# Pieces of projections between attention tiles, fewer stack transfers, and layer norms moved from ACT and DVE to POOL, in a two-layer transformer kernel on one core

## What is computed

```python
x = layernorm(x + attn(x))        # 16 heads, 2048 x 2048 scores each, softmax, w_out
dist = softmax(mean(x @ Wr + br)) # one row per batch
idx = sort(top_k(dist, 4))
Q, K, V = (x @ W + b for the four heads idx)
x = layernorm(x + softmax(Q K^T / 8) V @ Wo + bo)
def layernorm(x): return (x - mean) / sqrt(var + 1e-5)
```

## Time and profile before

| | us |
|---|---|
| median of 3 runs | 4086.33 (4085.86 to 4088.03) |
| the profiled execution | 4086.6 |
| its span, first to last instruction | 4084.8 |
| PE busy | 3616.2 (89%) |
| DVE busy | 3287.2 (80%) |
| ACT busy | 3098.1 (76%) |
| POOL busy | 1662.8 (41%) |
| mean granted TensorE clock | 0.887 of 2.4 GHz |

### The profile page before, as it was taken

The page is one execution under the profiler, slowest core; times in us unless marked ns, Lnnn a source line. Parts: engine busy times, 40 slices in busy tenths (PEclk is TensorE's granted clock), DMA queues, the critical chain, the costliest instruction groups (busy, mean ns, idle before and its releaser), DMA issues.

```text
span 4084.8 us, 41654 instructions
## 1 busy us (share of the span) xinstructions
PE 3616.2 (89%) x13992; PEld 1329.7 (33%) x13992; DVE 3287.2 (80%) x3352; ACT 3098.1 (76%) x5069; POOL 1662.8 (41%) x1115
## 2 busy tenths in 40 slices
PE   7888888778999999788999999788999999599997
PEld 3233223223333333323333332323333322343443
DVE  7888888988989898888989898888989898543442
ACT  5888888886888889786888889786888889423333
POOL 3122332100445555400445545401445545437776
PEclk7777777678999999878999999778999999799998
DMA  5122221110000000210000000210000000100000
GB/s 159 67 75 67 83 75 62 57 45 16 16 16 19 21 21 26 67 38 16 16 16 19 26 16 26 73 33 16 16 16 25 21 16 19 53 9 1 11 11 11
DMA packets 117192, 142.62 MB, mean 35 GB/s; under 512 B 33394, under 2 KB 100466, under 8 KB 116978
## 3 DMA queue, kind: packets, MB, share of 16 engines
q1 hardware_dynamic: 116978, 139.95, 11.0%
HBM read 89.55 MB, written 50.33 MB: 34 GB/s over the span
## 4 chain that ended last, share of the span: by engine, by line
PE 47%; DVE 29%; ACT 17%; issue 5%; POOL 2%; SPq 1%; DMA 0%; POOLq 0%; DVEq 0%; ACTq 0%
DVE nmax L1083 18%; ACT ps L920 14%; PE ps L796 8%; PE ps L886 8%; PE ps L858 7%; PE ps L761 7%; PE ps L873 7%; DVE smax L1162 6%; PE ps L775 6%; POOL facc L720 2%; PE ps L876 2%; PE ps L769 1%; PE ps L894 1%; ACT probs L990 1%; DVE st L1062 1%
## 5 line engine op out<-in xcount | busy, mean ns | idle before, releaser
L920 ACT ACTIVATE ps<-ps,nmax 128x1024 f32<-128x1024 f32 x2048 | 2233.0, 1094 | 388.4 <-DVE nmax L1083 365.6
L1083 DVE TENSOR_REDUCE nmax<-ps 128x1 f32<-128x1024 f32 x2048 | 2379.4, 1216 | 135.2 <-PE ps L796 122.5
L796 PE MATMUL ps<-stack 96*128 96x512 bf16 x4096 | 1350.6, 436 | 237.0 <-ACT ps L920 149.4
L720 POOL TENSOR_TENSOR facc<-facc,probs 128x1024 f32<-128x1024 f32 x448 | 1051.2, 2346 | 550.9 <-ACT probs L990 528.8
L1162 DVE TENSOR_REDUCE smax<-ps 128x2 f32<-128x1024 f32 x512 | 616.5, 1220 | 261.3 <-PE ps L858 260.9
L796 PEld LDWEIGHTS ps<-stack 96*128 96x128 bf16 x4096 | 298.2, 102 | 1411.0 <-ACT ps L920 939.2
L990 ACT ACTIVATE probs<-ps 128x1024 f32<-128x1024 f32 x512 | 524.0, 1024 | 229.1 <-PE ps L876 227.8
L858 PE MATMUL ps<-fk,fq 64*128 64x512 f32 x2048 | 571.0, 650 | 41.4 <-ACT ps L920 38.1
L873 PE MATMUL ps<-fq,fk 64*128 64x512 f32 x2048 | 545.7, 609 | 29.0 <-ACT ps L920 27.9
L886 PE MATMUL ps<-probs,vals 128*64 128x512 f32 x2048 | 506.9, 608 | 5.0 <-ACT probs L990 4.5
L920 ACT ACTIVATION_READ_ACCUMULATOR ps<-ps,nmax 128x1 f32 x2048 | 417.0, 204 | 0.0
(11 more groups left out here) (117 smaller groups left out, 1985.5 us busy)
## 6 DMA issues: line engine op xcount, KB each, us to landing
stack<-qk_levels SPq DMA_DIRECT2D x768, 64.0 KB, 2.2
qk_levels<-fk SPq DMA_DIRECT2D x64, 384.0 KB, 2.6
probs<-in_L_attn_x SPq DMA_DIRECT2D x16, 512.0 KB, 3.8
res<-in_L_attn_x SPq DMA_DIRECT2D x16, 512.0 KB, 4.0
v_rows<-vals SPq DMA_DIRECT2D x16, 512.0 KB, 2.6
vrows<-v_rows SPq DMA_DIRECT2D x16, 512.0 KB, 3.4
x_rows<-y SPq DMA_DIRECT2D x16, 512.0 KB, 2.9
res<-x_rows SPq DMA_DIRECT2D x16, 512.0 KB, 3.9
```

Source lines behind the costliest of these rows:

```text
L720: pool.tensor_tensor(total, total, probs[:, slot, :], ALU.add).then_inc(facc_ready, 1)
L796: last = pe.matmul(bank(banks[i]), stack[0:SK, hd % 2, 0, t * P:(t + 1) * P], stack[0:SK, hd % 2, 1, col:col + CH], start=True, stop=True)
L920: act.activation(src, src, ACT.Exp, bias=nmax[:, b % 2, half, t, hd:hd + 1], scale=-1.0, accum_out=esum[:, b % 2, half, t, hd:hd + 1]).the ...
L1083: dve.tensor_reduce(nmax[:, b % 2, half, t, hd:hd + 1], two_banks(banks), AX.XY, ALU.min).then_inc(min_ready, 1)
```

## The change

It has five parts, and the plan is computed anew with all of them.

- Projections are divided on PE: QP, KP, FK, FQ and D into two pieces, VP, FV, OP and FO into four (`PARTS`). Each piece is an entry of its own in PE's lists, at the same spot; the first takes the banks, the last tells the reader. Another unit can run between two pieces.
- A head's stack comes in six DMAs instead of 12: three for the queries, in which one level is repeated over up to three parts of the stack by a broadcast source, and three for the keys.
- In the last batch DVE adds the second to fourth bank of each group straight from PSUM to oacc; ACT's copy to part and POOL's addition are gone there.
- For both norms of batches 0 to 2 POOL computes the root, from an integer first guess (one step) and three Newton steps of four instructions, and scales. The last batch keeps ACT's root with one Newton step, and DVE.
- The order of the first inputs has each XT one chunk ahead of its projections, and the plan counts PE's units of the first stage at 1.5 times their cost (`COLD`).

```diff
+NEWTON = 3
+ROOT_START = float(0x5F3759DF)
+COLD = 1.5
+PARTS = {"QP": 2, "KP": 2, "FK": 2, "FQ": 2, "VP": 4, "FV": 4, "OP": 4, "FO": 4, "D": 2}
...
-    inputs += place([u for c in chunks for u in (("XT", 0, c), ("QP", 0, 0, c), ("KP", 0, 0, c))], -3, 1)
+    ahead = [("XT", 0, 0)]
+    for c in chunks:
+        ahead += [("XT", 0, c + 1)] * (c + 1 < NCH) + [("QP", 0, 0, c), ("KP", 0, 0, c)]
+    inputs += place(ahead, -3, 1)
...
+    for units in (main, inputs):
+        units[:] = [(spot, u) for spot, t in units for u in [("part", i) + t for i in range(PARTS.get(t[0], 1) - 1)] + [t]]
...
-        name = ("PE",) + tag
-        unit(name, us, after)
-        banks_of[name], reader[name] = banks, read_by
+        parts = PARTS.get(tag[0], 1)
+        for i in range(parts):
+            name = ("PE",) + (("part", i) if i + 1 < parts else ()) + tag
+            unit(name, us / parts, after if i == 0 else [])
+            banks_of[name] = banks if i == 0 else 0
+            if i == 0:
+                reader[name] = read_by
...
-        scale = dve if k == "OP" or b == B - 1 else pool
-        unit(act("LN", *t), 3.0, [dve(*t)])
-        unit(scale("NM", *t), 2.1 if scale is dve else 6.0, [act("LN", *t)])
+        scale = dve if b == B - 1 else pool
+        root = act if scale is dve else pool
+        unit(root("LN", *t), 3.0, [dve(*t)])
+        unit(scale("NM", *t), 2.1 if scale is dve else 4.9, [root("LN", *t)])
...
-                start(n, now, cost[n] + switch)
+                start(n, now, cost[n] * (COLD if key < 0 else 1) + switch)
...
-                    for side, which in ((0, Q_LEVEL), (1, K_LEVEL)):
-                        for g, lv in enumerate(which):
-                            sp.dma_start(stack[g * AD:(g + 1) * AD, k % 2, side, :],
-                                         qk_dram[b, side, h, lv, r * AD:(r + 1) * AD, :]).then_inc(stack_in[k % 2], 16)
+                    rows = qk_dram[b, :, h, :, r * AD:(r + 1) * AD, :]
+                    for at, n in ((0, 3), (3, 2), (5, 1)):
+                        into = lambda side: stack[at * AD:(at + n) * AD, k % 2, side, :]
+                        lv = Q_LEVEL[at]
+                        sp.dma_start(into(0), rows[0, lv:lv + 1].to_broadcast([n, AD, L])).then_inc(stack_in[k % 2], 16)
+                        sp.dma_start(into(1), rows[1, 0:n]).then_inc(stack_in[k % 2], 16)
...
+                elif kind == "LN":
+                    i, base = norm_no[at], (nth[n] - 1) * ROOT_STEPS
+                    pool.wait_ge(var_ready, i + 1)
+                    if i >= 2:
+                        pool.wait_ge(n_ready[i % 2], i // 2)
+                    pool.tensor_scalar(rstd[:, i % 2, :].bitcast(I32), var[:, i % 2, :].bitcast(I32), -0.5, ROOT_START,
+                                       ALU.mult, ALU.add).then_inc(newt_pool, 1)
+                    for k in range(NEWTON):
+                        pool.wait_ge(newt_pool, base + 4 * k + 1)
+                        newton(pool, i, newt_pool, base + 4 * k + 1, root_pool if k + 1 == NEWTON else newt_pool)
...
+                elif kind == "V":
+                    b, g, q = at
+                    dve.wait_ge(pv_done, step_no(b, g, (q + 1) * BURST - 1))
+                    dve.wait_ge(part_ready, nth["ACT", "V", b, g, 0])
+                    dve.wait_ge(oacc_ready, sum_no(b, g, q) - 1)
+                    dve.tensor_tensor(oacc[:, g % 2, :], bank(held["PE", "V", b, g, q * BURST][0]), oacc[:, g % 2, :],
+                                      ALU.add).then_inc(oacc_ready, 1)
```

More of the change, by code:

```diff
@@ L469, in build @@
         order, held, freed, planned = plan()
-        fill_no = {n[1:]: i + 1 for i, n in enumerate(n for n in order["PE"] if n in held and n[1] != "V")}
+        fill_no = {n[1:]: i + 1 for i, n in enumerate(n for n in order["PE"] if n in held and n[1] not in ("V", "part"))}
         nth = {}
@@ L495, in build @@
         norm_no = {t: i for i, t in enumerate(norms)}
-        nth_norm = [nth[e, "NM", *t] - 1 for t in norms for e in ("DVE", "POOL") if (e, "NM", *t) in nth]
         a_no = lambda b, j: b * A_TILES + j + 1
@@ L648, in scale_rows @@
             eng.wait_ge(steps, done + 3)
-            eng.tensor_tensor(r, r, n, ALU.mult).then_inc(steps, 1)
-            eng.wait_ge(steps, done + 4)
+            eng.tensor_tensor(r, r, n, ALU.mult).then_inc(last, 1)
+        def scale_rows(eng, i):
+            s = i % 2
             for t in range(TPC):
@@ L755, in _, with pieces, project_rows @@
             pe.wait_ge(wT_read, 3)
-            def project_rows(banks, rowsT, w):
-                for t in range(TPC):
+            def pieces(kind, piece, count):
+                parts = PARTS.get(kind, 1)
+                return range(count * piece // parts, count * (piece + 1) // parts)
+            def project_rows(kind, piece, banks, rowsT, w):
+                for t in pieces(kind, piece, TPC):
                     for cc in range(KC):
@@ L771, in transpose_rows, with project @@
                 last.then_inc(filled, 1)
-            def project(banks, wT, columns):
-                for cc in range(KC):
+            def project(kind, piece, banks, wT, columns):
+                for cc in pieces(kind, piece, KC):
                     last = pe.matmul(bank(banks[0]), wT(cc), columns(cc), start=(cc == 0), stop=(cc == KC - 1))
-                last.then_inc(filled, 1)
+                if cc == KC - 1:
+                    last.then_inc(filled, 1)
             for n in order["PE"]:
-                kind, at = n[1], n[2:]
-                banks = held.get(n)
+                if n[1] == "part":
+                    piece, kind, at = n[2], n[3], n[4:]
+                else:
+                    piece, kind, at = PARTS.get(n[1], 1) - 1, n[1], n[2:]
+                banks = held.get(("PE", kind) + at)
                 for was in freed.get(n, ()):
@@ L785, in _ @@
                         pe.wait_ge(y_ready, norm_no[was[1:]] + 1)
+                    elif was[:2] == ("DVE", "V"):
+                        pe.wait_ge(oacc_ready, sum_no(*was[2:]))
                     else:
@@ L806, in _ @@
                     pe.wait_ge(xT_ready, i + 1)
[L807 removed]
+                    project(kind, piece, banks, lambda cc: w_inT[:, cc, s * P:(s + 1) * P], lambda cc: xT[:, i % NCH, cc, :])
                 elif kind == "VP":
@@ L811, in _ @@
                     pe.wait_ge(xT_ready, i + 1)
-                    project_rows(banks, xT[:, i % NCH, :, :], w_inT[:, :, 2 * D:3 * D])
+                    project_rows(kind, piece, banks, xT[:, i % NCH, :, :], w_inT[:, :, 2 * D:3 * D])
                 elif kind == "OT":
@@ L819, in _ @@
                     pe.wait_ge(oT_ready, b * NCH + c + 1)
-                    project_rows(banks, oT, w_outT)
+                    project_rows(kind, piece, banks, oT, w_outT)
                 elif kind == "X1":
@@ L840, in _ @@
                     pe.wait_ge(wv_in, (b + 1) * V_DMAS * 16)
-                    project_rows(banks, x1T[:, :, c * CH:(c + 1) * CH], wv_sel)
+                    project_rows(kind, piece, banks, x1T[:, :, c * CH:(c + 1) * CH], wv_sel)
                 elif kind == "FO":
@@ L844, in _ @@
                     pe.wait_ge(foT_ready, group_no(b, PAIRS * c + PAIRS - 1) + 1)
-                    project_rows(banks, foT[:, :, c * CH:(c + 1) * CH], wo_sb)
+                    project_rows(kind, piece, banks, foT[:, :, c * CH:(c + 1) * CH], wo_sb)
                 else:
```

55 lines of the change are left out of this document (33 added, 22 removed).

## The result

The changed kernel takes 4099.00 us (median of ten runs, 4088.01 to 4101.36), beside 4086.19 (4085.28 to 4088.43) for the kernel before in the same series. The ratio is 1.0027 with a 95% interval of 1.0018 to 1.0036: a quarter of a per cent slower, where 2.5% faster was predicted. The profiled execution has a span of 4098.6 us, 13.8 more than before.

What follows compares the result with a forecast made beforehand. The first stage was taken as bound by DVE's work plus holes torn by whole projections, later stages by PE. Terms -4 - 42 - 42 - 9 - 3 - 4 = -104 us took 4086.6 to 3983 us, range 3915 to 4065.

Steps and rivals of the forecast that it cites:

- PE takes a tile between pieces whenever a pair of banks is free and the tile is due: First stage: tiles run between pieces of divided projections, so 60% of DVE's 70.3 us of waits go, -42 us.
- rival 5: Whole kernel: the plan shifts work but pieces come due together, time within 8 us of before; chance 0.05.
- The start: Before the first tile: transposes one chunk ahead and fewer stack DMAs to issue, -4 us, ends -7 and 0.
- The first stage: Batch 0's attention tiles, 60 to 711 us: divided projections close 60% of DVE's waits for VP and QP, -42 us.
- rival 1: PE is next at once: a third of the first stage's holes closes, -40 in all, 4047 us; chance 0.15.
- The wait for VP under 20 us: Sign of success in the first stage: DVE's wait before the VP copy falls from 47.5 to under 20 us.
- a mean clock under 0.6 in the first stage: Sign of being wrong: PE's mean granted clock in the first stage, 0.72 before, falls under 0.6.
- rival 3: First stage: cut-up runs keep PE at 1.2 GHz, deciding under mean clock 0.58; +110 us there, 4135 us; chance 0.08.
- The boundaries: Three stretches between PE-bound stages: division -11 and norms moved to POOL -3, so -14 each, -42 us in all.
- rival 2: POOL's longer norm chain sets the boundaries: -3 each, -9 for -42, 4016 us; chance 0.15.
- PE-bound stages: Three stages of the second attention: PE's idle time shrinks a little, -3 each, -9 us; ends -15 and +6.
- The last batch and the tail: From 3625 us on: DVE adds products from PSUM, -3 in the batch; three POOL additions leave the tail, -4.

Runs made afterwards that it cites:

- e3_whole: The changed kernel with all projections whole again (PARTS empty), all else as changed: 4115.31 us, ratio 1.0069 to the kernel before.
- e2_cold_one: The changed kernel with COLD at 1 in place of 1.5: 4081.14 us, ratio 0.9986 to the kernel before.
- f2_before_cold: The kernel before with only PE's first-stage work priced at 1.5 in the plan: 4097.40 us, ratio 1.0024.
- g1_apart_not_last: The changed kernel with twelve stack DMAs a head, COLD 1, and later pieces (except D's) at later spots, but not in the last batch: 4024.64 us.
- e1_twelve_dmas: The changed kernel with the old twelve stack DMAs a head in place of six: 4090.01 us, ratio 1.0004 to the kernel before.

## Why the prediction was wrong

**The step that failed** is the sentence "PE takes a tile between pieces whenever a pair of banks is free and the tile is due". It carries -42 us of the first stage and -33 of the boundaries. The plan takes the ready unit with the lowest spot, all pieces of a projection have one spot, and once the first is lower than the next tile, so are the rest. Only a piece taken ahead of its turn got another unit behind it. In the change 6 of the 112 pieces of QP, KP and VP that have a seam behind them are such, and none of the 6 got one; with COLD at 1 it is 48, of which 39 got one. Both the rule and the diff's "(spot, u) ... for u in" were in front of me. I had even named the case, as the bound "pieces come due back to back" and as rival 5, "The plan shifts the work but pieces come due together, so little changes", and gave it 0.05. Its mechanism is what happened in the first stage, where not one seam of QP, KP or VP was filled.

Point by point, forecast against what was measured:

- **The start**, -4: measured +4.2. The order of the transposes and the first issue did gain (first tile at 52.9 with twelve DMAs, 4.6 earlier: -4 was near for that part, though no run has the order alone). "If one costs the same to issue" missed the real cost. What mattered was not the issue but the transfer: three engines instead of sixteen. The issues were slower too, 0.4 to 0.9 us each and later 2.3 and 2.4. My upper bound for the start was 0, and a slower transfer was not in it.
- **The first stage**, -42: measured +23.3. The division gave 0 (e3_whole). What cost it is COLD, which I read as a detail of the order and gave no price: -20.7 when undone (e2_cold_one), +13.2 in the plan of before (f2_before_cold). With 66 of the 112 seams of that stage filled it is 23.3 us under before (g1_apart_not_last), about the third that rival 1 assumed, not the 60% that I took. So the term would have been nearly twice too large even with the mechanism at work in these seams. The wait for VP under 20 us that I named as a sign measured 23.2, but COLD brought it there and not the division: it is 23.2 in e3_whole too.
- **The clock**. The sign of being wrong was "a mean clock under 0.6 in the first stage": it rose, to 0.82. That does not test rival 3 yet, as the runs of VP were still whole. Cut up in g1_apart_not_last, the clock is 0.74, well over its 0.58, and rival 3 is out. But a higher clock was no gain: PE was quicker and then waited longer.
- **The boundaries**, -14 each: the periods, boundary and PE-bound stage together, gave -4.9, -6.9, -3.0, where -17 each was forecast. The holes before the norms and before the values' copy, which carried the -11, stayed as they were (13.6 and 9.9 us, before 12.2 and 10.0), since no seam of OP and FV was filled; with 13 and 21 of 48 filled, g1_apart_not_last waits 4.2 us for OP behind J1 and has no line for FV there. I summed division and norms (-3) as if each stood for itself. The norms alone give nothing; their lead is lost by the next J unless some pieces give as well.
- **POOL's chain**, rival 2: the 13 steps of 3.7 us and 4.8 us of scaling came as worked out (3.8 and 4.83), and PE's wait for y is 0.8 to 1.5 us in a boundary, under the 3 us that I had named. Rival 2 is out.
- **Table loads**: 64 before, 16 in the two lines of L1018 and L1020, as predicted, and ACT is 73 us less busy. It bought what the periods show and no more.
- **PE-bound stages**, -3 each: 0. From the first group's maximum to the next J it is 672.8, 672.9 and 672.4 us, before 672.7 in all three. So neither the -3 nor the +6 was seen.
- **The last batch and the tail**, -3 and -4: J3 to the end was +1.0. The part ahead of the first group's maximum became 2.8 longer (132.7, before 129.9), what follows it 1.8 shorter. Three lines of POOL's timeline in the tail show what was gained:

```profile
4038.71 2.35 POOL L752 TENSOR_TENSOR facc<-probs 128x1024 f32<-128x1024 f32 x1 [6.94 <-ACT probs L1036]
4041.20 34.74 POOL L755 TENSOR_TENSOR facc<-facc,probs 128x1024 f32<-128x1024 f32 x14
4079.94 0.61 POOL L769 COPY frec_wide<-frec 128x512 f32<-128x512 f32 x1 [4.00 <-DVE frec L1231]
```

The additions of oacc are gone from between those of facc, as predicted. From the first facc to the copy of frec it is 41.2 us, before 43.3 (4021.29 to 4064.60): 2.1 saved, not 3.8. Before, the third addition lay beside D's matmuls and cost nothing.

The ledger of the spans, forecast against found:

```
                          forecast   found
division, first stage        -42       0     e3_whole: tile stage 735.9, after 735.8
division, boundaries         -33     -17.0   whole periods, after less e3_whole
norms                         -9      +2.2   whole periods, e3_whole less before
PE-bound stages               -9       0     after less before, in the two rows above
COLD                           -      +20.7  e2_cold_one
rest of the tile stage         -      +2.6   e2_cold_one 715.1, before 712.5
start                         -4      +4.2   of it the wide DMAs +8.8, e1_twelve_dmas
last batch and tail           -7      +1.0
sum                         -104     +13.7
```

## What to carry to other kernels

When a change cuts work so that something else can run between the pieces, count in the written order how many seams are filled before giving the cut a price; a cut whose pieces all have the same priority is none wherever the first is taken in its turn, and a place in time for each piece was worth 32.6 us here (4057.26 to 4024.64). A factor in a planner is a part of the change like any other and wants a price and an experiment of its own. Before DMAs are merged into wider ones, look at what becomes outermost in them: here half as many DMAs brought the first tile 8.8 us later.

## What the hardware showed unexpectedly

- Stack DMAs with three or two levels outermost kept 3 of 16 DMA engines' worth busy (share 0.19, 76 GB/s); twelve a head with 16 rows outermost had 0.49 and 134 GB/s. On SP's queue the first six wide issues took 0.4 to 0.9 us each, the narrow ones 0.46 (11.10 us for 24). Six transfers with 16 rows outermost were not tried.
- Nearly the same PE work at a higher granted clock went with a longer stage: 497.1 us busy at 0.82 in the changed kernel, 559.7 at 0.72 with COLD undone, and the latter's stage is 20.7 us shorter.
- The norms' move gained nothing without division (+2.2 us in the periods), and with it the two gained 18.8 us. But e3_whole, whose boundary is 3.9 us shorter than that of before, has the same period of 914.8 us from J1 to J2 and from J2 to J3. What holds it at that value is open.
